# A float32 bias laid into the matmul's bank by ScalarE, in place of a matmul of ones

## The reference, cut to what matters

```python
xn = _layernorm(x, ln_g, ln_b)
x_t = xn @ W_up_l.T + b_up_l              # 256 wide
r_t = xn @ W_up_r.T + b_up_r              # 512 wide
x_c = silu(_causal_conv_feat(x_t, conv_w, conv_b))
x_skip = x_c @ W_skip.T + b_skip          # 512 wide: the skip projection
q, k, v, gates, o = ...                   # further projections of x_c and x_t
h = o * recurrence(q, k, v, gates)        # 8 heads of 64
hn = _layernorm(h.reshape(Bs, Sl, H, HD), mh_g, mh_b).reshape(Bs, Sl, HID)
out = (hn + x_skip) * silu(r_t)
return out @ W_down.T + b_down + x
```

## Time and profile before

| | |
|---|---|
| runs (median) | 427.73 us |
| profiled execution, its time | 427.93 us |
| its span | 425.7 us |
| TensorE (PE) busy | 378.5 us, 89% |
| VectorE (DVE) busy | 320.2 us, 75% |
| ScalarE (ACT) busy | 230.5 us, 54% |
| granted TensorE clock, mean | 0.953 |
| DMA moved | 46.10 MB |

### The profile page before, as it was taken

How to read it: one execution, slowest core, us unless ns; L and a number is a source line. 1 busy time by engine, 2 the same in 40 slices (tenths; PEclk the granted TensorE clock), 3 DMA queues, 4 the chain that set the end, 5 groups by cost and what they waited for, 6 DMA issues and landing times.

```text
span 425.7 us, 11362 instructions
## 1 busy us (share of the span) xinstructions
PE 378.5 (89%) x3607; PEld 300.8 (71%) x3629; DVE 320.2 (75%) x1042; ACT 230.5 (54%) x607; POOL 124.2 (29%) x125
## 2 busy tenths in 40 slices
PE   8149999999999999999999999999989868779990
PEld 5123799964687777877878878778768734579990
DVE  4892677766728898878989788988788995567870
ACT  3641344442556767567684567665556912555550
POOL 5475145531001111103110121111031068434552
PEclk9657999999999999999999999999999969899997
DMA  6997122219999999989600000000001612323320
GB/s 199 370 418 227 46 78 62 68 57 217 181 171 174 174 170 162 175 170 173 153 5 0 0 0 0 0 0 0 2 2 42 235 62 87 113 82 92 97 68 0
DMA packets 57265, 46.10 MB, mean 108 GB/s; under 512 B 4112, under 2 KB 53906, under 8 KB 56722
## 3 DMA queue, kind: packets, MB, share of 16 engines
q1 hardware_dynamic: 53618, 37.84, 42.0%
q0 software_dynamic: 2752, 5.73, 3.9%
q10 hardware_dynamic: 864, 2.15, 1.6%
HBM read 17.99 MB, written 27.25 MB: 106 GB/s over the span
## 4 chain that ended last, share of the span: by engine, by line
PE 63%; DVE 12%; ACT 8%; issue 6%; DMA 3%; POOL 3%; another core or an unknown queue 1%; SPq 0%; DVEq 0%; POOLq 0%; ACTq 0%
PE bank L918 59%; ACT WVT L796 4%; POOL slots L521 2%; DVE ST L1450 1%; PE bank L1288 1%; ACT E L805 1%; PE bank L1055 1%; DMA XN<-slots 1%; ACT W1R L816 1%; DMA slots<-XN,POS 1%; DVE QS L2001 1%; ACT XNT L736 1%; DMA QKT<-by_token 1%; DMA by_token<-YB,IDX 1%
## 5 line engine op out<-in xcount | busy, mean ns | idle before, releaser
L569 POOL TENSOR_TENSOR HS<-HS,MHALF 128x8 f32<-128x8 f32 x16 | 26.4, 1647 | 130.9 <-DVE HS L2051 130.9
L918 PE MATMUL bank<-XBT,W1R 128*128 128x128 f32 x368 | 50.1, 280 | 0.5 <-ACT XBT L691 0.4
L918 PE MATMUL bank<-W,HT 128*128 x368 | 49.0, 276 | 0.7 <-issue 0.7
L918 PEld LDWEIGHTS bank<-XBT,W1R 128*128 128x128 f32 x368 | 45.3, 194 | 1.7 <-ACT XBT L691 1.4
L918 PEld LDWEIGHTS bank<-W,HT 128*128 128x128 f32 x368 | 44.8, 192 | 1.2 <-issue 0.8
L698 ACT ACTIVATE HT<-bank,W1R 128x128 f32<-128x128 f32 x115 | 34.8, 366 | 16.2 <-PE bank L918 12.5
L796 ACT ACTIVATE WVT<-bank,AC 128x128 f32<-128x128 f32 x128 | 36.6, 376 | 11.8 <-PE bank L918 11.7
L521 POOL DMA_INDIRECT slots<-XN,POS x32 | 32.6, 1018 | 19.4 <-issue 13.0
L918 PE MATMUL bank<-MASKB,IDB 128*128 128x512 bf16 x130 | 35.4, 398 | 3.0 <-POOL HS L569 1.2
L760 ACT ACTIVATE QKT<-bank,COLS 128x512 f32<-128x512 f32 x32 | 22.0, 687 | 29.0 <-PE bank L918 29.0
L550 POOL DMA_INDIRECT by_token<-YB,IDX x23 | 22.0, 958 | 30.3 <-DVE YB L1713 29.9
(11 more groups left out here) (363 smaller groups left out, 972.4 us busy)
## 6 DMA issues: line engine op xcount, KB each, us to landing
slots<-FILL SPq DMA_DIRECT2D x74, 258.0 KB, 7.9
W<-w SPq DMA_DIRECT2D x2, 2048.0 KB, 10.6
XN<-slots SPq DMA_DIRECT2D x23, 129.0 KB
W<-w SPq DMA_DIRECT2D x1, 2064.0 KB
slots<-QKT SPq DMA_DIRECT2D x1, 1483.5 KB, 6.2
XB<-slots SPq DMA_DIRECT2D x23, 64.5 KB
X<-x SPq DMA_DIRECT2D x4, 256.0 KB, 5.3
QKT<-by_token SPq DMA_DIRECT2D x4, 256.0 KB, 4.0
```

The lines of the kernel that those rows point to most:

```text
L569: g.tensor_tensor(HS[:, 3, :], HS[:, 2, :], MHALF[:, 0:H], ALU.pow).then_inc(roots_ready, 1)
L918: return t_.matmul(o, l, r, start=start, stop=stop, skip_group_check=True)
```

## The change

The skip's bias becomes a float32 row on all 128 partitions (`ROWS` grows by 512 values for each partition, `BROWS` shrinks by 512 on one). VectorE adds `mh_b` to it once, over 128 partitions. `SKIPB`, `ONESR` and the seven instructions that made them go. ScalarE, after reading bank 1 for `k2` or for `o` of chunks 1 to 3, waits for its own read, copies the bias row into the bank and only then counts `pj_free`. The skip projection's first product goes and its six others add onto what lies in the bank.

```diff
-BROW = {"bv": 0, "bo": 512, "br": 1024, "bsk": 1536}
-ROW = {"mhb": 0, "mhg": 512, "bdown": 1024, "cw": 1152, "cb": 1156}
-NBROW, NROW = 2048, 1157
+BROW = {"bv": 0, "bo": 512, "br": 1024}
+ROW = {"bsk": 0, "mhb": 512, "mhg": 1024, "bdown": 1536, "cw": 1664, "cb": 1668}
+NBROW, NROW = 1536, 1669
...
-            sp.dma_start(BROWS[0:1, :], rowpack[0:NBROW].unsqueeze(0)).then_inc(cols_loaded, 16)
+            sp.dma_start(BROWS[0:1, 0:NBROW], rowpack[0:NBROW].unsqueeze(0)).then_inc(cols_loaded, 16)
...
+            def skip_bias(n, i):
+                act.wait_ge(bank_read, n + 1)
+                return a.activation(PJ[i][:, :], row("bsk", HID), ACT.Copy)
...
-                a.activation(QKT[:, m, :], PJ[i][:, :], ACT.Identity, bias=col("bq", m)).then_inc(pj_free[i], 1)
+                ins = a.activation(QKT[:, m, :], PJ[i][:, :], ACT.Identity, bias=col("bq", m))
+                if use == "k2":
+                    ins.then_inc(bank_read, 1)
+                    ins = skip_bias(NC * b, i)
+                ins.then_inc(pj_free[i], 1)
...
-                    a.activation(OT[:, c % 2, :], PJ[i][:, :], ACT.Tanh, scale=0.5).then_inc(pj_free[i], 1)
+                    ins = a.activation(OT[:, c % 2, :], PJ[i][:, :], ACT.Tanh, scale=0.5)
+                    if c:
+                        ins.then_inc(bank_read, 1)
+                        ins = skip_bias(NC * b + c, i)
+                    ins.then_inc(pj_free[i], 1)
...
-                if what == "s":
-                    mm(dst[:, :], ONESR[:, :], SKIPB[:, :], True, False)
...
-                do(v.memset(SK23[0:65, 0, :], 0.0))
-                do(v.tensor_tensor(SK23[0:1, 0, :], row("bsk", HID)[0:1, :], row("mhb", HID)[0:1, :], ALU.add))
-                do(v.tensor_copy(SKIPB[:, :], SK23[0:65, 0, :]))
-                did(v.tensor_copy(ONESR[:, :], const("ones")[0:65, :]))
-                do(v.tensor_tensor(SK23[0:1, 0, :], SK23[0:1, 0, :], SKIPB[0:1, :].bitcast(F32), ALU.subtract))
-                do(v.tensor_copy(SKIPB[64:65, :], SK23[0:1, 0, :]))
-                v.memset(CREDIT[:, 11:12], 0.0).then_inc(skip_bias_ready, 1)
+                v.tensor_tensor(row("bsk", HID), row("bsk", HID), row("mhb", HID), ALU.add).then_inc(skip_bias_ready, 1)
```

More of the change, by code:

```diff
@@ L169, in macaron @@
         MASKB = sb("MASKB", [P, 512], BF16)
-        SKIPB = sb("SKIPB", [65, HID], F32R)
         SK23 = sb("SK23", [P, 2, HID])
-        ONESR = sb("ONESR", [65, P], F32R)
         SELQ = sb("SELQ", [P, NC, H * P], BF16)
@@ L317, in macaron @@
         folds_ready, fold_full, folds_split = sem("folds_ready"), sem("fold_full"), sem("folds_split")
-        skip_bias_ready = sem("skip_bias_ready")
+        skip_bias_ready, bank_read = sem("skip_bias_ready"), sem("bank_read")
         attn_consts = sem("attn_consts")
```

## The result

The changed kernel takes 432.55 us (median of 4 runs, 430.87 to 434.48); the kernel before, run beside it, takes 427.86 us (median of 4, 426.88 to 428.43). The ratio is 1.0134, with a 95% interval of 1.0102 to 1.0167. It is slower by 4.7 us, and 432.8 had been forecast. The profiled execution of the changed kernel took 434.48 us, with a span of 432.3. "Take o" is ScalarE's tanh of the `o` projection, printed `XN<-bank`; E is the tile of its four exponentials behind it; QS is VectorE's product of the queries with E, for which TensorE's `from_state` waits.

A forecast was written before the change was run, and what follows sets the result against it. Two nearly tied chains, TensorE's own products and take o, E, QS over ScalarE and VectorE, meet at `from_state`. Profiled 427.93 + 4.4 (sequences) + 0.0 (head) + 0.6 (opening) = 432.9, forecast as 432.8 us; 8-in-10 range 426.8 to 435.6.

The forecast's parts named there:

- What TensorE saves: In the skip projections, sixteen bias products go at 0.23 us each, worth 3.7 us if nothing else is late.
- What ScalarE's copy costs: Behind take o, a copy of 0.61 us holding ScalarE 0.48; E starts 1.12 after take o.
- Chunks: `from_state` late by 0.16 us in chunk 0, 0.33 in all in chunk 1, 1.1 in chunk 2; chunk 3 gives nothing back.
- Head: At each sequence's start, behind k2, gain and wait cancel: 0.0 us, or 0.1 lost if the copy takes 0.70.
- The sign that was named: QS's lateness should show as TensorE's wait ahead of `from_state`, 0.3 to 0.8 us each; under 0.1 would refute the prediction.
- The far bounds: For ScalarE's copy: at 0.26 us the four sequences cost 2.0; at 1.2 a sequence costs about 2.8, so 11.
- The opening: Longer ROWS lands K 0.63 to 0.71 us later, moving everything to the first expert block about 0.6; bounds 0 and 1.2.
- A: Rival: TensorE's stream alone is the bound, copies hide, 3.7 us go: 424.8, or 424.2 without the opening; chance 0.12.
- B: Rival: gain and cost cancel, VectorE's chunk 1 lateness given back before chunk 2; sequence costs 0 to 0.4, 427.9 to 430.1; chance 0.15.
- C: Rival: ScalarE's copy into a bank takes 0.9 us or more; a sequence costs 2.0 or more, 436.5 and above; chance 0.07.
- D: Rival: more gaps on TensorE could lower its granted clock; no size given, no chance of its own.

The follow-up runs named there:

- e1: The changed kernel without ScalarE's sixteen copies, so the skip gets no bias and no bias product; 424.52 us, ratio 0.9970 to the kernel before.
- e11: The changed kernel with the sixteen copies written to an unread SBUF tile, without the wait for the own read; skip without bias; 429.04 us, ratio 1.0053.
- e10: The changed kernel with the copies of chunks 1 to 3 moved behind E's four exponentials in ScalarE's order; 440.46 us, ratio 1.0331.
- e6: The changed kernel with only the skip of chunk 1, made in chunk 0, laid by ScalarE; the others keep the bias product; 427.39 us, ratio 1.0015.
- e7: The changed kernel with only the skip of chunk 2, made in chunk 1, laid by ScalarE; the others keep the bias product; 431.16 us, ratio 1.0104.
- e5: The changed kernel with only the head's skip (chunk 0, behind k2) laid by ScalarE; chunks 1 to 3 keep the bias product; 426.21 us, ratio 0.9986.
- e9: The changed kernel with each copy 128 in place of 512 columns wide, the other 384 getting no bias; 429.08 us, ratio 1.0052.
- e4: Against the kernel before, no bias product and no copy into PSUM; GpSimd adds the bias row onto the skip in SBUF; 433.39 us, ratio 1.0156.
- e8: The changed kernel with only the skip of chunk 3, made in chunk 2, laid by ScalarE; the others keep the bias product; 429.39 us, ratio 1.0070.

## Why the prediction was right

**What TensorE saves.** Right in price (0.23 for each product, e1's step 0 to 1 and head), and right that most of chunk 2's is not to be had. One reading was off: the pace of 0.23 was used up to `from_state` (132.37), but the step from the last product to it is 0.32 in the kernel before, so TensorE's own products set the start in all three chunks. The chain over QS was ready 0.33 sooner in chunks 0 and 1 and 0.05 sooner in chunk 2, counting the 0.06 from QS to `from_state` that the changed kernel shows. The prediction's 0.07 and 0.10 for this last step stand in none of its rows.

**What ScalarE's copy costs.** I took 0.61 and it is 0.60. The hold, the time from its start to the start of the next instruction, I took as 0.48 and it is 0.53 (130.83 to 131.36). E is 1.18, 1.18 and 1.15 behind take o in place of 1.12. The Trainium skill ("ScalarE: Activation LUTs", "Step-by-step: what each stage is for") says that ScalarE reaches PSUM with less latency than SBUF. No run here shows it cleanly: 0.60 into the bank in the changed kernel and 0.62 to 0.67 into SBUF in e11 point that way, but the copies of e10 into the bank, which overlap the instruction ahead of them as those of e11 do, take 0.62 to 0.68, and the hold is 0.52 in both. Of the overlap of about 93 ns between activations that the same page of the Trainium skill gives ("What ACT_TABLE_LOAD costs") the changed kernel shows 0.60 - 0.53 = 0.07 behind the copy, and e11 shows 0.62 - 0.48 = 0.14 behind take o; for the copy the page was nearer than the row I used.

**Chunks.** Chunk 0 was forecast 0.16 late and is 0.20 (e6's 0.19); chunk 1 another 0.17 and is 0.23; chunk 2 another 0.77 and is 0.73. The chain through VectorE, which in chunk 1 carries the lateness to L2048 and the squares, is shown by e7. Its parts were larger than forecast and partly made up for at the end: counted from take o of chunk 0, L2048 is 0.76 later (forecast 0.65), E of chunk 2 is 1.28 later (1.11), and `from_state` 1.16 (1.10), since the four exponentials took 1.12 in place of 1.19, and QS had been ready 0.05 too early in the kernel before. Chunk 3 gives nothing back (12.36 and 12.35), as forecast. Head: forecast 0.0, with 0.1 if the copy were longer; it is 0.07 longer in e5. The copy was not longer, but the second product of the skip starts 0.33 behind the first one (181.34 and 181.67), where the pace is 0.23.

**The sign that was named.** TensorE was to wait 0.3 to 0.8 ahead of `from_state` in each chunk. Against the kernel before it is idle 0.21 more there, in each of the three. So the account had the right order of the two chains and too much room between them: six products behind the copy were to end 0.37 ahead of `from_state`, and they end 0.21 ahead of it. TensorE's own chain, by its wait for bank 1, is nearly as late as the one over QS.

**The far bounds.** The quarter copy was put at some 0.5 for each sequence; e9 has 0.21. The upper end of 2.8 leaves out the head, where a copy of 1.2 would have cost about 0.6 more by the prediction's own numbers. Neither moves the forecast.

**The opening.** This step failed. It forecast that K lands 0.65 later and that everything to the first expert block moves with it by 0.6. K was used about 0.4 later, L1820 started 0.23 later, and the first expert block came at 44.24, 0.64 earlier. In the 13 profiles its place goes with the time at which the granted clock rises from 1.2 to 2.4 GHz in the folds, and not with the length of the row:

| profiles | clock rises | TensorE's products ahead of it end | first expert block |
|---|---|---|---|
| changed, e5, e6 | 31.3 to 31.9 | 41.3 to 41.7 | 43.3 to 44.2 |
| before, e1 to e4, e9 to e11 | 35.1 to 37.5 | 42.6 to 44.3 | 43.7 to 44.9 |
| e7, e8 | 42.0 and 42.3 | 46.3 and 46.6 | 46.1 and 46.4 |

In the five that have the rise at 37.1 to 37.5, these products end at 44.21 to 44.27, the kernel before with its short row among them (44.24). In the first group the gain of the early rise is not kept: TensorE is idle for 2.0 to 2.5 ahead of the first block, for VectorE or for the DMA of XB, and the clock falls again for 3.4 us from 45.0 to 45.6. This group has the longest time from the first expert block to the first `from_state`, 88.8 to 89.1, where the others have 86.7 to 88.5. Why the rise comes when it does stays open. Two experiments that differ only in which place ScalarE lays, much later, differ in it by 10.7 us (same columns as above; first e6, then e8):

```profile
28.00:34.00 6.00, 5.66 (x10) 2.18 (x10) 5.13 (x32) 0.38 (x1) 4.57 (x5) 0.72 0.98 398
34.00:44.00 10.00, 7.62 (x28) 2.99 (x27) 3.61 (x12) 1.85 (x4) 4.79 (x5) 1.00 0.54 192
44.00:52.00 8.00, 8.00 (x57) 8.00 (x58) 4.44 (x18) 3.60 (x12) 1.30 (x2) 0.79 0.14 38
```
```profile
28.00:34.00 6.00, 6.00 (x8) 2.30 (x9) 4.88 (x30) 0.38 (x1) 4.78 (x5) 0.50 1.00 407
34.00:44.00 10.00, 10.00 (x20) 3.19 (x19) 1.68 (x8) 0.69 (x2) 3.89 (x5) 0.60 0.53 182
44.00:52.00 8.00, 7.74 (x56) 6.17 (x55) 5.22 (x19) 3.69 (x12) 0.86 (x1) 1.00 0.06 17
```

In e6 the clock is at 2.4 GHz from 31.3 us, TensorE is done early, idles for 2.01, and the clock is at 1.2 GHz from 45.0 to 48.4; in e8 it is at 1.2 GHz until 42.0. The first `from_state` of all profiles lies between 130.85 and 133.52. Against that, 0.2 to 0.6 of K can't be seen in the time.

**The sum.** Forecast 4.4 for the sequences and 0.6 for the opening; measured 4.9 for the mLSTM layer in the profile and 4.7 in the medians. The total is right partly by luck: the sequences cost 0.1 more each than forecast while the opening's term did not appear. That the median came within 0.3 of the forecast says little, since the four runs lie 3.6 apart.

**The rivals.** A is excluded by the sequence of e1, B by the steps (nothing is given back before chunk 2), C by the 0.60 of the copy. D: in the changed kernel the granted clock was 1.00 from the first `from_state` to the last; it moved in the opening and again behind 352.8. In e10, with longer waits, it fell in a sequence.

## What to carry to other kernels

Before work is moved off the busiest engine, look at which chain reaches the next meeting point last and by how much: here the second chain came 0.05 to 0.33 us behind the first. So taking four products of 0.23 from the first was worth 0.50 a sequence and not 0.92, and laying the bias on the second cost 1.72, measured against the kernel with neither. ScalarE was 54% busy, and still had no free place at the ones tried: what stood behind the new instruction in its queue was awaited. A chain that starts late on an engine without gaps (VectorE in chunk 1) brings the lateness back one chunk later, at a place that the edit did not touch.

## What the runs showed of the hardware

- A ScalarE copy of 128x512 float32 from SBUF takes 0.60 us into a bank when it starts behind the end of the instruction ahead of it (changed kernel), 0.62 to 0.68 into a bank (e10) and 0.62 to 0.67 into SBUF (e11) when it starts before that end. Ahead of another activation that waits for nothing it holds the engine 0.54, 0.52 and 0.52.
- ScalarE's wait for its own read costs 0.17 us: the copy starts 0.65 behind take o with it (130.18 to 130.83, changed kernel) and 0.48 without (196.98 to 197.46, e11).
- A 128x512 float32 addition in SBUF takes GpSimd 1.26 to 1.50 us (e4). Beside the eight additions into tile SK, seven times a VectorE operation of 0.69 began while GpSimd's ran; it took 1.66 to 1.79 and ended 0.55 behind GpSimd's end. By the rows VectorE got next to nothing done until GpSimd was through. An operation of VectorE that was already running when GpSimd started was not slowed (0.68). A small one was caught as well: 128x4 took 0.83, 0.17 as a rule.
- The granted clock rose between 31 and 42 us in the opening, in kernels whose instructions up to there were almost the same, and runs of one kernel were up to 6 us apart (e1: 422.95 to 429.12). The first three sequences of one profile agreed within 0.25, but for e10, where the clock was at 1.2 GHz for 3.4 us of the first. For an effect of a few tenths of a percent, the profile's steps tell more than the medians.
